# First mixture's loop: places' parts and late constants ahead of the wait for low activations, bias rows at the sixth scattering

## The chip, the cores and the metric

One core of a Trainium2 chip runs the whole program in one launch. The metric is device microseconds of that core, the median over runs. A profiled execution gives its own time, its span and a trace of every engine: PE (TensorE matmuls), PEld (its weight loads), DVE (VectorE), ACT (ScalarE), POOL (GpSimd) and the DMA queues.

## The reference

The program is a decoder of four layers over a batch of 8 sequences of 128 tokens with 128 features (1024 tokens). Each layer is an attention or recurrence, then a feed-forward part, each with layer norm and a gated residual. The change is in the feed-forward part of the first layer, a mixture of 8 experts in which each token goes to one expert:

```python
def _L0_ffn_ref(x, Wr, br, W1, b1, W2, b2):
    xf = x.reshape(-1, D)
    expert_idx = jnp.argmax(xf @ Wr.T + br, axis=-1)
    h = jax.nn.relu(jnp.einsum('td,efd->etf', xf, W1) + b1[:, None, :])
    y = jnp.einsum('etf,edf->etd', h, W2) + b2[:, None, :]
    return y[expert_idx, jnp.arange(xf.shape[0])].reshape(B, S, D)
...
x = x + jnp.tanh(g_xattn[0]) * _L0_xattn_ref(_layernorm(x), ...)
x = x + jnp.tanh(g_ffn[0]) * _L0_ffn_ref(_layernorm(x), ...)
```

The hidden width is 512. After this part come the second layer's attention and six more parts, which the change does not touch.

## The kernel before

The engines' programs are written out by hand, each in its own order, and joined by semaphores. An engine runs its own list in order, so an instruction that waits holds back everything that stands behind it in the list.

In the first mixture the tokens are sorted by expert into 15 tiles of 128 slots (1920 slots; each expert's last tile may be partly empty). Values are split into a high and a low fp16 piece, and a product is three matmuls (high by high, high by low, low by high). What matters of it:

- **Places and parts.** DVE compares each token's place with the slot numbers and so writes a 0/1 matrix for a chunk of 512 slots, in eight parts, one for each batch (`pick_dve`, L1373; its result is `PICK`, two buffers). There are four chunks, the last of 384 slots. PE multiplies the tokens' rows by the parts (`gather_pe`, L1415): for each chunk eight matmuls for the high pieces and eight for the low ones. The matmul of the high pieces for batch b waits for part b. ACT copies the result out (`gather_act`, L1423). Chunks 0 and 1 are made before the loop, 2 and 3 in it.
- **The loop over 15 tiles.** Turn i has on PE: the second layer of tile i (`tile_down_pe`, 12 matmuls), the scattering of tile i - 2 back to token order (`tile_scatter_pe`, 16 matmuls into two PSUM banks that collect all tiles), the first layer of tile i + 3 (`tile_up_pe`, 12 matmuls), and in turns 3, 4, 7 and 8 one half of a gathering (`GATHER_AT`: chunk 2 in turns 3 and 4, chunk 3 in turns 7 and 8). All but the gathering have the line of the helper `products`, L228.
- **ACT in turn i:** the high piece of tile i's result (`tile_y_act`, L1482), four relu's of tile i + 3 (L1453) and their high piece (L1458), and in the turns of `GATHER_AT` the copy of the gathered half.
- **DVE in turn i:** the low piece of tile i's result (`tile_y_dve`, L1486), the 0/1 matrix by which tile i is scattered (`put_dve`, L1401), a group of late constants in the turns of `LATE_AT` (`late_dve`, L352 to L390: high and low pieces of weights and biases and masks, most of them for later stages), the low piece of tile i + 3's activations (`tile_low_dve`, L1462), which waits for ACT's high piece, and behind it, in turns 0 to 7, two parts of `pick_dve`.
- **Second-layer bias.** PE adds it for all tokens at once, ahead of the first scattering (turn 2): 16 matmuls of 8 rows on `B2H` and `B2L`. They wait for `b_split` at 3, which group 0 of the late constants brings (L355 to L358, turn 1).

Of the kernel before, what the change touches and what calls it, by code (L numbers as in the profile page):

```python
# [8 lines left out]
NB, S, D = 8, 128, 128  # L9
TOK = NB * S  # L10
HALF = TOK // 2
F0, E0 = 512, 8
# [5 lines left out]
TILES = TOK // 128 + E0 - 1  # L18
# [22 lines left out]
def gated_mix_program(nc, t, out):  # L41
# [5 lines left out]
    with ctx:  # L47
        def sb(name, shape, dt=fp32):
            return ctx.enter_context(nc.sbuf_tensor(name, shape, dt))
# [3 lines left out]
        def sem(name):  # L53
            if name not in sems:
                sems[name] = ctx.enter_context(nc.semaphore(name))
            return sems[name]
# [36 lines left out]
        B2F, B2H, B2L = sb("B2F", [E0, D]), sb("B2H", [E0, D], fp16), sb("B2L", [E0, D], fp16)  # L93
# [5 lines left out]
        CT = sb("CT", [128, TOK], fp16)  # L99
# [32 lines left out]
        def bank(i, n=1):  # L132
            return PS[:, 512 * i:512 * (i + n)]
# [91 lines left out]
        def products(pe, dst, pairs, start=True, stop=True):  # L225

            for i, (l, r) in enumerate(pairs):
                last = pe.matmul(dst, l, r, start=start and i == 0, stop=stop and i == len(pairs) - 1)  # L228
            return last
# [66 lines left out]
        def weights_low(eng, n, q):  # L296

            eng.wait_ge(sem("s_w_high"), 4 * n + q + 1)
            if n == 1:
                eng.wait_ge(sem("s_w"), 2 + q)  # L300
            hi, lo = (w[:, quarter(q), :].rearrange("p e n -> p (e n)") for w in ((W1H, W1L), (W2H, W2L))[n])
            signal = "s_w_pool" if n == 0 and q < 2 else "s_w"
            eng.tensor_tensor(lo, staged(n, q), hi, ALU.subtract).then_inc(sem(signal), 1)
# [976 lines left out]
        def part(c):  # L1280
            return min(512, SLOTS - 512 * c)
# [25 lines left out]
        def rows_dve(dve):  # L1307
            for i in range(2):
                h = slice(4 * i, 4 * i + 4)
                dve.wait_ge(sem("s_copied"), i + 1)  # L1310
                dve.tensor_tensor(XNL[:, h, :], XN[:, h, :], XNH[:, h, :], ALU.subtract).then_inc(sem("s_row_low"), 1)

        def places_dve(dve):

            at = [ROUTED]

            def step(ins):
                at[0] += 1
                ins.then_inc(sem("r0_step"), 1)
                dve.wait_ge(sem("r0_step"), at[0])  # L1320

            step(dve.tensor_tensor(R_LESS, over(IOTA[:], E0), along(IOTA[:], E0), ALU.is_lt))
            dve.wait_ge(sem("s_ranks"), 1)
            step(dve.tensor_tensor(R_OVER, along(bank(2)[:, 0:E0], 8), over(IOTA[:], E0), ALU.is_gt))
            step(dve.tensor_reduce(R_N, R_OVER, AX, ALU.add))
            step(dve.tensor_tensor(R_SUM, over(R_N, E0), R_LESS, ALU.mult))
            step(dve.tensor_reduce(R_AT, R_SUM, AX, ALU.add))
            ranks = bank(3)[:, 0:NB * E0].rearrange("p (b e) -> p b e", b=NB)
            step(dve.tensor_tensor(R_RANK, ranks, over(R_AT, NB), ALU.add))
            step(dve.tensor_tensor(R_OWN, R_RANK, CW[:, :, 0:E0], ALU.mult))  # L1330
            step(dve.tensor_reduce(R_POS, R_OWN, AX, ALU.add))
            assert at[0] == POSITIONS

        def tiles_dve(dve):

            at = [POSITIONS]

            def step(ins):
                at[0] += 1
                ins.then_inc(sem("r0_step"), 1)  # L1340
                dve.wait_ge(sem("r0_step"), at[0])

            dve.wait_ge(sem("ld_late"), 16 * len(LATE))
            step(dve.tensor_tensor(R_TILE, over(R_AT, 16), along(SLOT[:, 0:16], E0), ALU.is_lt))
            step(dve.tensor_reduce(R_EX, R_TILE, AX, ALU.add))
            step(dve.scalar_tensor_tensor(R_EXF, R_EX, -1.0, SLOT[:, 16:32], ALU.add, ALU.mult))
            step(dve.tensor_reduce(R_SUM8, R_EXF.rearrange("p (g t) -> p g t", g=2), AX, ALU.add))
            dve.tensor_copy(R_EXI, R_SUM8).then_inc(sem("r0_step"), 1)
            assert at[0] == EXPERTS - 1

        def bias_dve(dve):

            dve.tensor_scalar(R_OH, R_EX[0:E0], 1 / 128, SLOT[0:E0, 0:1], ALU.mult, ALU.is_equal).then_inc(sem("r0_step"), 1)
# [11 lines left out]
        def pick_dve(dve, c, batches=range(NB)):  # L1365

            if c == 1:
                dve.wait_ge(sem("s_w_pool"), 2)
            if c >= 2:
                dve.wait_ge(sem("s_gathered"), 2 * c - 2)  # L1370
            n = part(c)
            for b in batches:
                dve.tensor_scalar(PICK[c % 2][:, b, 0:n], STEP[:, 0:n], 4.0 * c, R_POS[:, b:b + 1], ALU.add, ALU.is_equal)\  # L1373
                    .then_inc(sem("s_pick"), 1)
# [20 lines left out]
        def put_dve(dve, i):  # L1395

            if i >= 2:
                dve.wait_ge(sem("s_scattered"), i - 1)
            else:
                dve.wait_ge(sem("s_copied"), 5 + NB)  # L1400
            dve.tensor_scalar(PUT[:, i % 2, :], PLACE, SLOT[:, i:i + 1], None, ALU.is_equal).then_inc(sem("s_put"), 1)  # L1401
# [58 lines left out]
        def tile_low_dve(dve, i):  # L1460
            dve.wait_ge(sem("s_high"), i + 1)
            dve.tensor_tensor(LOWS[i % 3], RH[i % 3], HIGHS[i % 3], ALU.subtract).then_inc(sem("s_low"), 1)  # L1462
# [21 lines left out]
        def tile_y_dve(dve, i):  # L1484
            dve.wait_ge(sem("s_y_high"), i + 1)
            dve.tensor_tensor(YL[:, i % 2, :], bank(4 + i % 2)[:, 0:128], YH[:, i % 2, :], ALU.subtract)\  # L1486
                .then_inc(sem("s_y_low"), 1)

        def tile_scatter_pe(pe, i):

            if i == 0:
                pe.wait_ge(sem("r_ct"), 1)
                pe.wait_ge(sem("b_split"), 3)
                for b in range(NB):
                    products(pe, bank(b // 4)[:, 128 * (b % 4):128 * (b % 4) + 128],
                             [(CT[0:E0, 128 * b:128 * b + 128], b2[:]) for b2 in (B2H, B2L)], start=b % 4 == 0, stop=False)
            pe.wait_ge(sem("s_put"), i + 1)
            pe.wait_ge(sem("s_y_low"), i + 1)
            for b in range(NB):
                last = products(pe, bank(b // 4)[:, 128 * (b % 4):128 * (b % 4) + 128],  # L1500
                                [(PUT[:, i % 2, 128 * b:128 * b + 128], y[:, i % 2, :]) for y in (YH, YL)],
                                start=False, stop=i == TILES - 1 and b % 4 == 3)
                if i == TILES - 1 and b % 4 == 3:
                    last.then_inc(sem("y_turned"), 1)
            if i < TILES - 1:
                last.then_inc(sem("s_scattered"), 1)

# [46 lines left out]
                    gather_act(act, *GATHER_AT[i])  # L1554

        GATHER_AT = {3: (2, (0,)), 4: (2, (1,)), 7: (3, (0,)), 8: (3, (1,))}
        LATE_AT = (1, 4, 5, 6, 8, 9, 10, 11, 12)

        def moe0_dve(dve):
            rows_dve(dve)  # L1560
            places_dve(dve)
            pick_dve(dve, 0)
            tiles_dve(dve)
            bias_dve(dve)
            for q in (2, 3):
                weights_low(dve, 0, q)
            pick_dve(dve, 1)
            for q in range(3):
                weights_low(dve, 1, q)
            tile_low_dve(dve, 0)  # L1570
            weights_low(dve, 1, 3)
            tile_low_dve(dve, 1)
            tile_low_dve(dve, 2)
            for i in range(TILES):
                tile_y_dve(dve, i)
                put_dve(dve, i)
                if i in LATE_AT:
                    late_dve(dve, LATE_AT.index(i))
                if i + 3 < TILES:
                    tile_low_dve(dve, i + 3)  # L1580
                if i < 8:
                    at = 2 * (i % 4)
                    pick_dve(dve, 2 + i // 4, range(at, at + 2))

        def moe_loads(sp, m):
            if m == 0:
# [987 lines left out]
```

## Time and profile before

| | |
|---|---|
| Median of 3 runs | 644.99 us (644.38 to 647.12) |
| Profiled execution: time, span | 648.96 us, 647.2 us |
| Busy share: PE, DVE, ACT, POOL | 88%, 80%, 53%, 39% |
| Mean granted clock of TensorE | 0.959 of full speed |
| Loop over tiles, by PE | 74.3 to about 129 us |

The page gives the span in 40 slices of 16.2 us; the loop lies in slices 5 to 8. A row of the timeline gives the start, the duration, the engine, the line, the operation, output and inputs, how many instructions of the sort lie together, and in brackets how long the engine was idle before it and what ended the idle time. PE's durations overlap one another, so PE's pace is read from the distance of starts.

### The profile page before, as it was taken

Reading aid. Unit: us, or ns where it says so; the run is one execution under the profiler, and the core shown is the slowest. Engines: PE = TensorE matmul, PEld = TensorE weight load, DVE = VectorE, ACT = ScalarE, POOL = GpSimd, SP = SyncE. Lnnn points to the kernel's source line nnn. Section 1 sums busy time; section 2 is a strip of 40 time slices with the busy share of each in tenths; the row PEclk is TensorE's granted clock in tenths of the full one; section 3 lists DMA queues with packets and bytes.
Section 4 is the critical chain, followed back from the end, with each engine's and each line's share of the span. In section 5 each row is a group of like instructions: output and inputs, shape, how many; then the busy total and the mean of one; then the engine's idle time right before and its main releaser. Section 6 shows DMA issues by size and latency. Waiting matters only on the chain.

```text
span 647.2 us, 16313 instructions
## 1 busy us (share of the span) xinstructions
PE 567.3 (88%) x5394; PEld 292.8 (45%) x5394; DVE 518.1 (80%) x1136; ACT 340.5 (53%) x675; POOL 249.4 (39%) x456
## 2 busy tenths in 40 slices
PE   4899888987977789967999999999999779996897
PEld 2444567834653345533444344343434325553443
DVE  6798845696889868856799999999999796766886
ACT  4778735664654533433455555555555454333554
POOL 3474000210584068773244444344443100234462
PEclk9999978996998999987899999999999899997999
DMA  8500200060000000001466665666666000001110
GB/s 324 196 2 2 68 3 3 2 151 2 4 2 1 2 1 3 2 3 36 134 180 172 168 172 171 166 177 178 177 169 170 27 2 2 2 3 30 31 53 34
DMA packets 34912, 48.89 MB, mean 76 GB/s; under 512 B 6756, under 2 KB 26800, under 8 KB 34472
## 3 DMA queue, kind: packets, MB, share of 16 engines
q1 hardware_dynamic: 34424, 47.40, 25.8%
q8 instruction: 37, 0.61, 0.4%
q10 hardware_dynamic: 432, 0.73, 0.3%
q14 instruction: 19, 0.16, 0.1%
HBM read 47.29 MB, written 0.82 MB: 74 GB/s over the span
## 4 chain that ended last, share of the span: by engine, by line
PE 43%; DVE 41%; ACT 7%; issue 4%; POOL 3%; DMA 1%; DVEq 0%; ACTq 0%; SPq 0%; POOLq 0%
PE PS L228 30%; DVE PS L1115 8%; DVE SHARED L1264 4%; DVE SHARED L1788 4%; PE PS L2020 2%; DVE PS L1128 2%; ACT SHARED L1093 2%; PE PS L2026 2%; ACT SHARED L1064 2%; PE PS L1892 2%; DVE MB L1914 2%; DVE PS L1914 2%; DVE STAT L394 2%; DVE REC L2034 1%; DVE XN L410 1%
## 5 line engine op out<-in xcount | busy, mean ns | idle before, releaser
L228 PE MATMUL PS<-XH,UH 128*128 128x512 f16 x232 | 91.0, 392 | 5.4 <-DVE PS L1115 3.3
L1093 ACT ACTIVATE SHARED<-PS 128x512 f16<-128x512 f32 x96 | 57.1, 597 | 72.5 <-DVE PS L1128 67.7
L228 PE MATMUL PS<-XL,UH 128*128 128x512 f16 x232 | 90.1, 389 | 0.0
L228 PE MATMUL PS<-XH,UL 128*128 128x512 f16 x232 | 90.0, 388 | 0.0
L2001 ACT ACTIVATE SHARED<-PS 128x512 f32<-128x512 f32 x96 | 52.1, 594 | 64.0 <-PE PS L228 48.8
L228 PE MATMUL PS<-SHARED,DNH 128*128 128x512 f16 x232 | 69.0, 379 | 4.6 <-DVE SHARED L1264 3.7
L1064 ACT ACTIVATE SHARED<-PS 128x512 f32<-128x512 f32 x96 | 57.2, 597 | 20.1 <-PE PS L228 15.1
L1264 DVE TENSOR_TENSOR SHARED<-PS,SHARED 128x512 f16<-128x512 f32 x96 | 62.0, 687 | 6.8 <-ACT SHARED L1093 3.4
L1022 POOL CAST DNH<-DF 128x128 f16<-128x128 f32 x58 | 19.6, 338 | 119.7 <-DMA DF<-in_down 95.0
L1128 DVE TENSOR_TENSOR PS<-PS,SHARED 128x512 f32<-128x512 f32 x92 | 59.7, 695 | 3.8
L1115 DVE TENSOR_TENSOR PS<-SHARED,PS 128x1024 f32<-128x1024 f32 x46 | 56.6, 1230 | 6.7 <-PE PS L228 0.7
L1914 DVE TENSOR_REDUCE MB<-PS 128x4 f16<-128x512 f32 x64 | 41.1, 688 | 17.0 <-PE PS L228 11.0
L2005 POOL TENSOR_TENSOR SHARED<-SHARED,GPT 128x512 f32<-128x512 f32 x32 | 40.0, 1273 | 24.3 <-ACT SHARED L2001 24.3
L1781 ACT ACTIVATE SHARED<-PS,LOB,LOM 128x512 f16<-128x512 f32 x48 | 35.4, 775 | 26.0 <-PE PS L228 26.0
L228 PEld LDWEIGHTS PS<-XH,UH 128*128 128x128 f16 x232 | 23.1, 99 | 50.8 <-DVE PS L1115 24.6
L228 PE MATMUL PS<-SHARED,DNL 128*128 128x512 f16 x116 | 44.1, 380 | 0.0
L1015 POOL TENSOR_TENSOR UL<-UF,UH 128x256 f16<-128x256 f32 x58 | 38.9, 671 | 4.6
L2020 PE MATMUL PS<-SHARED,ONE 128*32 128x128 f32 x768 | 40.5, 284 | 0.0
L2026 PE MATMUL PS<-SHARED,V 128*32 128x128 f32 x768 | 39.4, 277 | 0.6 <-POOL SHARED L2005 0.6
L1788 DVE SCALAR_TENSOR_TENSOR SHARED<-PS,BQK,SHARED 128x512 f16<-128x512 f32 x48 | 33.6, 740 | 6.0 <-ACT SHARED L1781 5.9
L228 PEld LDWEIGHTS PS<-SHARED,DNH 128*128 128x128 f16 x232 | 22.2, 98 | 33.6 <-issue 7.1
L228 PEld LDWEIGHTS PS<-XH,UL 128*128 128x128 f16 x232 | 23.2, 100 | 29.1 <-issue 3.0
(345 smaller groups left out, 1285.8 us busy)
## 6 DMA issues: line engine op xcount, KB each, us to landing
SHARED<-w_rows_dram SPq DMA_DIRECT2D x31, 384.0 KB, 3.7
SHARED<-w_rows_dram SPq DMA_DIRECT2D x30, 256.0 KB, 3.7
UF<-in_up SPq DMA_DIRECT2D x58, 128.0 KB, 3.4
SHARED<-w_rows_dram SPq DMA_DIRECT2D x31, 128.0 KB, 2.9
DF<-in_down SPq DMA_DIRECT2D x58, 64.0 KB, 2.9
V<-in_up SPq DMA_DIRECT2D x2, 1024.0 KB, 8.3
SHARED<-in_down SPq DMA_DIRECT2D x4, 512.0 KB
SHARED<-t_values_dram SPq DMA_DIRECT2D x2, 1024.0 KB, 10.4
```

Of the source, the lines that this page charges most:

```text
L228: last = pe.matmul(dst, l, r, start=start and i == 0, stop=stop and i == len(pairs) - 1)
L1064: act.activation(SG1[u][:, hf, :], bank(hf), ACT.Silu).then_inc(sem("e_act"), 1)
L1093: act.activation(HHI[:, u, hf, :], bank(4 + hf) if m == 1 else HF[:, hf, :], ACT.Copy).then_inc(sem("e_high"), 1)
L1115: dve.tensor_tensor(dst, SG1[u].rearrange("p i n -> p (i n)"), bank(2, 2), ALU.mult).then_inc(sem("w1_gated"), 1)
L1128: dve.tensor_tensor(bank(4 + hf), bank(4 + hf), WB[u][:, HALF * hf:HALF * hf + HALF], ALU.mult)\
L1264: dve.tensor_tensor(HLO[:, u, hf, :], src, HHI[:, u, hf, :], ALU.subtract).then_inc(sem("e_low"), 1)
L1788: dve.scalar_tensor_tensor(dst, proj_bank(a, "kq", e), BQK[:, a, "qk".index(c), g:g + 1], TLO[:, e % 4, :], ALU.add, ALU.subtract).then_in ...
L1914: dve.tensor_reduce(dst, src, AX, ALU.max, negate=True).then_inc(sem("a_max"), 1)
L2001: act.activation(PF[:, j, :], bank(2 + j % 2), ACT.Exp).then_inc(sem("a_exp"), 1)
L2005: pool.tensor_tensor(PG[:, j, :].rearrange("p (g s) -> p g s", g=4), PF[:, j, :].rearrange("p (g s) -> p g s", g=4), over(GPT[:, b, :], 4) ...
L2020: pe.matmul(bank(4 + u)[32 * g:32 * g + 32, 128:256], ONE8[:, j, :], PF[:, j, 128 * g:128 * g + 128], start=j == 0, stop=j == 3, skip_grou ...
L2026: last = pe.matmul(bank(4 + u)[32 * g:32 * g + 32, 0:128], V32[:, b, 4 * g + j, :], src[:, j, 128 * g:128 * g + 128], start=False, stop=j ...
```

## The change

DVE's parts move from the end of a turn to the place between `put_dve` and the late constants, that is ahead of `tile_low_dve` and its wait. They are dealt out 3, 3 and 2 over turns 0 to 2 (chunk 2) and over turns 4 to 6 (chunk 3), in place of 2 in each of turns 0 to 7. The first four groups of late constants move from turns 1, 4, 5 and 6 to turns 3, 4, 6 and 7; the other five stay. On PE the bias matmuls move from ahead of the first scattering (turn 2) to behind the sixth (turn 7), with their waits; the first scattering now opens the two banks, and the sixth signals the end of its last bias matmul.

```diff
         def tile_scatter_pe(pe, i):
-            if i == 0:
-                pe.wait_ge(sem("r_ct"), 1)
-                pe.wait_ge(sem("b_split"), 3)
-                for b in range(NB):
-                    products(pe, bank(b // 4)[:, 128 * (b % 4):128 * (b % 4) + 128],
-                             [(CT[0:E0, 128 * b:128 * b + 128], b2[:]) for b2 in (B2H, B2L)], start=b % 4 == 0, stop=False)
             pe.wait_ge(sem("s_put"), i + 1)
             pe.wait_ge(sem("s_y_low"), i + 1)
             for b in range(NB):
                 last = products(pe, bank(b // 4)[:, 128 * (b % 4):128 * (b % 4) + 128],
                                 [(PUT[:, i % 2, 128 * b:128 * b + 128], y[:, i % 2, :]) for y in (YH, YL)],
-                                start=False, stop=i == TILES - 1 and b % 4 == 3)
+                                start=i == 0 and b % 4 == 0, stop=i == TILES - 1 and b % 4 == 3)
                 if i == TILES - 1 and b % 4 == 3:
                     last.then_inc(sem("y_turned"), 1)
+            if i == 5:
+                pe.wait_ge(sem("r_ct"), 1)
+                pe.wait_ge(sem("b_split"), 3)
+                for b in range(NB):
+                    last = products(pe, bank(b // 4)[:, 128 * (b % 4):128 * (b % 4) + 128],
+                                    [(CT[0:E0, 128 * b:128 * b + 128], b2[:]) for b2 in (B2H, B2L)], start=False, stop=False)
             if i < TILES - 1:
                 last.then_inc(sem("s_scattered"), 1)
...
-        LATE_AT = (1, 4, 5, 6, 8, 9, 10, 11, 12)
+        PICK_AT = {0: (2, range(0, 3)), 1: (2, range(3, 6)), 2: (2, range(6, 8)),
+                   4: (3, range(0, 3)), 5: (3, range(3, 6)), 6: (3, range(6, 8))}
+        LATE_AT = (3, 4, 6, 7, 8, 9, 10, 11, 12)
...
                 tile_y_dve(dve, i)
                 put_dve(dve, i)
+                if i in PICK_AT:
+                    pick_dve(dve, *PICK_AT[i])
                 if i in LATE_AT:
                     late_dve(dve, LATE_AT.index(i))
                 if i + 3 < TILES:
                     tile_low_dve(dve, i + 3)
-                if i < 8:
-                    at = 2 * (i % 4)
-                    pick_dve(dve, 2 + i // 4, range(at, at + 2))
```

## Rows read from the trace of the kernel before

**Rows 1.** The page: TensorE's granted clock in 40 slices

```profile
PEclk9999978996998999987899999999999899997999
```

**Rows 2.** Waits from 60 to 130 us: who <- for whom: us, times, longest

```profile
PE PS L1415 <- DVE V L1373: 1.9, 1, 1.9
...
PE PS L1415 <- DVE SHARED L1373: 1.6, 1, 1.6
PE PS L228 <- DVE B2L L358: 1.5, 1, 1.5
```

**Rows 3.** Busy time in stretches of the loop, with the granted clock (PEclk)

```profile
core 0: us, PE busy (x) PEld busy (x) DVE busy (x) ACT busy (x) POOL busy (x), PEclk, DMA share, GB/s
80.10:85.70 5.60, 4.08 (x44) 3.92 (x45) 3.27 (x11) 0.96 (x3) 0.00 (x0) 0.70 0.01 3
85.70:91.50 5.80, 4.22 (x51) 3.01 (x49) 3.11 (x9) 3.71 (x11) 0.95 (x1) 1.00 0.00 1
91.50:97.50 6.00, 6.00 (x50) 4.56 (x50) 1.54 (x5) 2.58 (x7) 0.00 (x0) 0.72 0.01 3
97.50:104.90 7.40, 7.40 (x122) 6.91 (x121) 6.03 (x20) 5.02 (x15) 0.98 (x1) 1.00 0.01 3
104.90:113.80 8.90, 7.02 (x59) 5.12 (x57) 3.52 (x11) 4.14 (x12) 0.00 (x0) 0.81 0.01 2
```

**Rows 4.** Timeline of DVE, turns 0 to 3, a pair of chunk 3, after the loop

```profile
66.42 2.17 DVE L1373 TENSOR_SCALAR V<-QX,SHARED 128x512 f16<-128x512 f16 x8
...
76.06 0.48 DVE L1401 TENSOR_SCALAR SHARED<-SHARED,REC 128x1024 f16<-128x1024 f16 x1
78.60 0.69 DVE L1462 TENSOR_TENSOR SHARED<-SHARED 128x512 f16<-128x512 f32 x1 [2.06 <-ACT SHARED L1458]
...
80.32 0.57 DVE L352 CAST WH<-WF 128x804 f16<-128x804 f32 x1
...
81.60 0.67 DVE L1462 TENSOR_TENSOR SHARED<-SHARED 128x512 f16<-128x512 f32 x1
...
90.63 0.61 DVE L1373 TENSOR_SCALAR SHARED<-QX,SHARED 128x512 f16<-128x512 f16 x2
...
98.21 0.55 DVE L1373 TENSOR_SCALAR V<-QX,SHARED 128x384 f16<-128x384 f16 x2
...
129.09 0.75 DVE L1697 SCALAR_TENSOR_TENSOR X<-PS,G,X 128x512 f32<-128x512 f32 x1 [1.58 <-PE PS L228]
```

**Rows 5.** Timeline of PE: a whole gathering, turn 2, the halves' first six matmuls

```profile
69.09 3.62 PE L1415 MATMUL PS<-V,CF 128*128 128x512 f16 x16
...
78.96 0.22 PE L228 MATMUL PS<-W2H,SHARED 128*128 x1
...
81.62 0.21 PE L228 MATMUL PS<-B2H,CT 8*128 8x128 f16 x1 [1.53 <-DVE B2L L358]
...
87.99 1.47 PE L1415 MATMUL PS<-SHARED,CF 128*128 128x512 f16 x6
...
104.85 1.14 PE L1415 MATMUL PS<-V,CF 128*128 128x384 f16 x6
```

**Rows 6.** Busy time in single turns without gathering (6, 7 but its gathering, 9, 11)

```profile
99.71:102.29 2.58, 2.58 (x44) 2.33 (x41) 2.17 (x8) 2.02 (x6) 0.98 (x1) 1.00 0.04 10
102.29:104.85 2.56, 2.56 (x41) 2.32 (x41) 2.56 (x10) 2.05 (x6) 0.00 (x0) 1.00 0.00 0
113.77:116.01 2.24, 2.24 (x43) 2.23 (x40) 0.80 (x2) 0.97 (x3) 0.00 (x0) 1.00 0.00 0
...
118.51:121.24 2.73, 2.70 (x44) 2.35 (x41) 2.49 (x12) 2.05 (x6) 0.00 (x0) 1.00 0.02 6
```

**Rows 7.** Timeline of ACT: the high piece of tile 4

```profile
80.18 0.63 ACT L1458 ACTIVATE SHARED<-SHARED 128x512 f16<-128x512 f32 x1
```

**Rows 8.** The chain that ended last: products of turns 0 and 1

```profile
74.32 1.19 PE PS L228 x12
...
75.65 1.09 PE PS L228 x12
```

## The prediction

> **What bounds the kernel now.** I looked first at the page's slices of the granted clock [rows 1]: within the loop over tiles the clock is not full in slices 5, 6 and 7. Then I asked for the waits of that stretch. PE has three there that end with a DVE instruction, 1.9, 1.6 and 1.5 us [rows 2]: one on the low piece of the second-layer bias, two on a part of a chunk. The timeline says where. The bias matmul starts at 81.62 after 1.53 us of idleness; the gathering of chunk 2 does six matmuls at 87.99 and then stands, and that of chunk 3 does six at 104.85 and stands [rows 5]. In both it is the last pair of parts, the one of turn 3 (DVE at 90.63) and the one of turn 7, that is late [rows 4]. Last I cut the loop into stretches [rows 3]. PE is idle 5.60 - 4.08 = 1.52, 5.80 - 4.22 = 1.58 and 8.90 - 7.02 = 1.88 us in three of them, 4.98 together, and not at all in the others. The clock is at 0.70, 0.72 and 0.81 in 80.1 to 85.7, 91.5 to 97.5 and 104.9 to 113.8, and 1.00 between. With the two levels of 1.2 and 2.4 GHz, 0.70 over 5.60 us is 3.36 us at the lower level, 0.72 over 6.00 is 3.36, and 0.81 over 8.90 is 3.38. Each came just after one of the three idle times, and each loses half its length: 1.68 + 1.68 + 1.69 = 5.05 us.
>
> So in the loop PE is the bound wherever it is not waiting, and DVE is the one that it waits for, though DVE itself is idle much of the time: it stood 2.06 us in front of the low piece of tile 3 [rows 4], with two parts queued behind, and the parts needed nothing that was late. An in-order queue has put work that is ready behind a wait.
>
> **The change part by part.**
>
> *Bias to the sixth scattering.* The wait of 1.53 us before the first scattering goes. What then holds the first scattering? Its matrix was written at 76.06 + 0.48 [rows 4] and the low result before that, so nothing: PE goes on from tile 2's second layer, begun at 78.96 [rows 5], at about 80.1. The 16 matmuls are no fewer: at full clock I take the pace of the turns, below, about 0.055 us each, 0.9 us together, in turn 2 or in turn 7 alike; this term is zero. The new place waits for `b_split` from turn 3 of DVE, four turns earlier: no wait. Behind it stand tile 10's first layer and the high half of chunk 3, 0.9 us later than otherwise, which only helps the parts.
>
> *Parts ahead of the low piece.* Eight parts of 512 slots took 2.17 us, 0.27 each; a pair of 384 slots 0.55 or less, so 0.24 to 0.27 each [rows 4]. In turn 0 three parts go from 76.5 to 77.3, into the idle 2.06 us before 78.60: free. In turn 1 DVE writes result and matrix from 79.2 to 79.8 and three parts to 80.6; the high piece of tile 4 ends at 80.81 [rows 7], so free again, and its low piece comes at 80.9, earlier than the 81.60 of now. In turn 2 the result waits for the first scattering, about 81.0; DVE takes it at 81.5 and ends the last two parts at 82.7. PE meanwhile: second layer of tile 2 to 80.1, scattering 81.0, first layer 81.8, turn 3 in some 2.6 us [rows 6] to 84.4, then the gathering. The seventh part is wanted six matmuls later, at 84.4 + 6 x 0.22 = 85.7 (16 took 3.62 us [rows 5]). Margin: 3.0 us. The second stall goes, 1.58.
>
> For chunk 3 the parts lie in turns 4 to 6. DVE gets to turn 6's result about 2.9 us after PE begins that turn (PE's turn of 2.6, then relu's and high piece hold the low piece before it), and ends two parts 0.6 + 0.5 us later, at +4.0. PE begins the gathering of turn 7 at 2.6 + 2.6 + 0.9 (bias) = +6.1, so the seventh part has a margin of over 2 us. The third stall goes, 1.88.
>
> *Late constants.* Group 0 lasts from 80.32 to 81.60, 1.28 us [rows 4], and now stands in turn 3 in front of the low piece of tile 6, which PE wants three turns later. DVE's heaviest turns become 4 and 6, with 0.2 + 0.4 (result, matrix) + 0.7 or 0.5 (parts) + about 1 (constants) + 0.6 (low piece) = 2.9 us at most, against PE turns of 2.6 + 1.8 and 2.6. The excess of 0.3 us in turn 6 is covered by turns 5 and 7, which have less on DVE and more on PE. Cost 0; were the cover gone, 0.3 us.
>
> *Clock.* With no idle time in this stretch, the three falls should not come. This is where I choose: the stretch 97.5 to 104.9, PE busy without a gap, kept 1.00 [rows 3], and so I take the whole 5.05 for the profiled execution. The lower bound is 0.
>
> *The sum,* first way: 1.52 + 1.58 + 1.88 + 5.05 = 10.0. Second way, a walk over turns 2 to 8: the turns without a gathering last 2.58, 2.56, 2.24 and 2.73 [rows 6]; their mean is 2.53, times seven 17.7; the half gatherings 1.8 + 1.8 + 1.4 + 1.4 = 6.4 (a chunk of 384 at three quarters); bias 0.9. That is 25.0, so turn 9 starts at 78.96 + 25.0 = 104.0 where it starts at 113.77 now [rows 6]: 9.8. With all turns at 2.24 it is 11.8, with all at 2.73 8.4. I take 9.8: the profiled 648.96 would be 639.2. The end of the loop has nothing of fixed time: from turn 9 all engines follow PE, and the next attention begins when the last scattering ends.
>
> The median of the timed runs is 4.0 us under the profiled execution, so some idle or low-clock time of this trace may be missing in them. The stalls are of the order of the queues and stay, 5.0; of the clock's 5.05 I count five sixths, 4.2. Gain 9.2: **644.99 - 9.2 = 635.8**.
>
> *A rule against it.* Two of the four turns of [rows 6] give 2.58 and 2.73 us for 40 matmuls, 65 to 68 ns each. The Trainium skill (TensorE: Matmul & The Clock Gate, Back-to-back issue gap) gives about 81 ns for a sustained stream of matmuls of 128 columns. By that figure a turn would be an estimated 3.2 us and seven turns some 5 us longer; the trace does not agree in any turn at full clock.
>
> **The rivals.**
>
> *A. The clock stays low.* The falls come from the thin stretches of short products in the loop and not from the gaps. For: 0.70 began while PE had been working again for some time. Against: 97.5 to 104.9, the same work, at 1.00 [rows 3]. Gain 5.0: 640.0. The same page (Why this matters for your kernels) ties a fall to gaps longer than these three; by it they would not be the cause.
>
> *B. PE's own pace.* With no stalls, PE never finds its instructions lying ready. In turns 0 and 1, 24 matmuls with weights picked by register took 1.19 + 1.09 us, 95 ns each [rows 8]. If all seven turns went so, one would last 2.28 + 0.9 (scattering) = 3.18 us, 0.65 more than the mean, 4.5 in all. Gain 9.8 - 4.5 = 5.3: 639.7. Against: turns 6 and 7 follow each other without a stall, at 2.58 and 2.56 [rows 6].
>
> *C. The third stall stays,* because DVE, with constants and parts before each low piece, falls behind in turns 4 to 6. Gain 10.0 - 1.88 - 1.69 = 6.4: 638.6. It wants a delay of over 2 us where I find 0.3.
>
> *D. Given back:* the loop ends sooner and the next stage waits for something of its own, or falls in other places for the clock. 643 to 646.
>
> *E. Slower.* The parts now stand between the high piece and the low piece of each tile; if the second layer wants the low piece at once, 8 x 0.27 + 8 x 0.24 = 4.1 us come onto the path and a wait on low pieces takes the place of each stall: 649.1. It decides where the low piece ends later than PE reaches the tile. Tile 3's ends at 79.3 and PE comes for it at 81.8, so 2.5 us would have to be lost against parts of 0.8.
>
> **How the numbers follow.** My forecast (633 to 638.2) 0.66, A 0.12, B 0.08, C 0.06, D 0.04, E 0.04. About 0.5%, 3.2 us, is what a measurement of this kernel can tell from no change. Faster by more than that: 0.66 + 0.12 + 0.08 + 0.06 = 0.92, less 0.02 for a run of small misses: 0.90; same 0.06; slower 0.04. The range goes from 632.5 (turns at the quick pace, all falls gone) to 641.0, which takes in A, B and C and leaves out D and E and 0.1 for the rest.
>
> **What the profile after would show.** PE without a wait on L1373 or L358 in the loop; a granted clock of 1.00 from 74 to about 119; DVE's parts ahead of L1462 in turns 0 to 2 and 4 to 6; the last gathering ending near 103.5 and the first L1697 near 119.3 in place of 129.1 [rows 4]. I am wrong if PE waits for L1462 (E), if parts are still late in turn 7 (C), if the clock falls between 80 and 105 with no gap before it (A), or if turns last 3 us at full clock (B).

## The result and the profile after

The changed kernel takes 636.99 us (635.60 to 639.53, 4 runs) against 644.68 us (644.38 to 647.12, 4 runs): ratio 0.9887, 95% interval 0.9853 to 0.9920. The profiled execution took 636.67 us with a span of 634.9 us. Six more runs in a second comparison gave 637.07 us and a ratio of 0.9904 (0.9868 to 0.9939).

The page of the changed kernel, the granted clock; slices are 15.9 us here, the loop lies in slices 5 to 8:

```profile
PEclk9999999987998799979999999999999899997999
```

The low slices within the loop [rows 1] are gone. The same loop in stretches (columns as in [rows 3]; from the scattering of turn 2 to the gathering of turn 3; that gathering and turns 4 and 5; turns 6 to 8 with chunk 3; the rest):

```profile
80.36:84.51 4.15, 4.15 (x69) 3.79 (x67) 3.09 (x10) 3.07 (x9) 0.00 (x0) 1.00 0.02 6
84.51:92.43 7.92, 7.92 (x99) 6.03 (x97) 6.16 (x19) 5.14 (x14) 1.32 (x1) 1.00 0.01 3
92.43:104.20 11.77, 11.77 (x168) 10.01 (x166) 8.87 (x26) 8.29 (x25) 1.06 (x1) 1.00 0.01 3
104.20:119.10 14.90, 14.90 (x228) 13.13 (x226) 10.17 (x26) 8.52 (x24) 4.37 (x4) 1.00 0.01 2
```

PE is busy in every microsecond from 80.4 to 119.1. Where [rows 3] have 4.08 of 5.60 and 7.02 of 8.90, stretch and busy time are now one number, and the clock is 1.00. Of PE's waits from 74 to 119 us [rows 2] this is all that is left; it is the wait for the second layer's weights that stands ahead of the loop in both kernels:

```profile
PE PS L228 <- DVE SHARED L303: 1.0, 1, 1.0
```

DVE's timeline, turns 0 to 2 and the turns with chunk 3, answers to [rows 4]:

```profile
76.77 0.87 DVE L1373 TENSOR_SCALAR SHARED<-QX,SHARED 128x512 f16<-128x512 f16 x3
78.91 0.69 DVE L1462 TENSOR_TENSOR SHARED<-SHARED 128x512 f16<-128x512 f32 x1 [1.27 <-ACT SHARED L1458]
...
80.12 0.87 DVE L1373 TENSOR_SCALAR SHARED<-QX,SHARED 128x512 f16<-128x512 f16 x3
81.16 0.69 DVE L1462 TENSOR_TENSOR SHARED<-SHARED 128x512 f16<-128x512 f32 x1 [0.17 <-ACT SHARED L1458]
...
82.37 0.61 DVE L1373 TENSOR_SCALAR SHARED<-QX,SHARED 128x512 f16<-128x512 f16 x2
...
85.55 1.04 DVE L355 CAST BH<-BF 4x128 f16<-4x128 f32 x1
...
92.93 1.54 DVE L1373 TENSOR_SCALAR V<-QX,SHARED 128x384 f16<-128x384 f16 x3
...
95.67 0.54 DVE L1373 TENSOR_SCALAR V<-QX,SHARED 128x384 f16<-128x384 f16 x2
...
119.15 0.75 DVE L1698 SCALAR_TENSOR_TENSOR X<-PS,G,X 128x512 f32<-128x512 f32 x1 [1.58 <-PE PS L228]
```

DVE still waits for ACT, 1.27 us in turn 0 where it was 2.06, but nothing that PE needs soon is queued behind. The last pair of chunk 2 is ready at 83.0 and its first part wanted at about 85.8; the last pair of chunk 3 is ready at 96.2 and wanted at about 99.6. Two rows were not expected, a cast of 4 x 128 of 1.04 us and three parts in 1.54 us; they come back below.

I measure the loop from the first matmul of tile 0's second layer to DVE's first update of x. Before it is 74.32 to 129.09, 54.77 us; after, 74.63 to 119.15, 44.52 us. That is 10.25 us in the traced executions, against some 7 in the medians. Where the rest went is what the experiments are about.

### The profile page after: what moved, and what is told of

The parts are those of the page before. It is cut to its first block, busy times and chain, and to the rows that moved or that the text cites. A ratio compares the mean times of both kernels' runs of the same rounds, so it can differ in the third digit from the quotient of the medians.

```text
span 634.9 us, 16313 instructions
## 1 busy us (share of the span) xinstructions
PE 562.7 (89%) x5394; PEld 289.0 (46%) x5394; DVE 518.2 (82%) x1136; ACT 340.1 (54%) x675; POOL 249.3 (39%) x456
## 4 chain that ended last, share of the span: by engine, by line
PE 44%; DVE 41%; ACT 6%; issue 4%; POOL 3%; DMA 1%; DVEq 0%; ACTq 0%; POOLq 0%
PE PS L228 29%; DVE PS L1115 9%; DVE SHARED L1264 5%; DVE SHARED L1789 4%; DVE PS L1128 3%; PE PS L2021 2%; ACT SHARED L1093 2%; PE PS L2027 2%; DVE MB L1915 2%; ACT SHARED L1064 2%; PE PS L1893 2%; DVE REC L2035 1%; DVE PS L1915 1%; DVE STAT L394 1%; DVE XN L410 1%
```

## The experiments

A row of the whole loop gives its length, PE's busy time and the granted clock at once. All such rows below have the columns of [rows 3].

### The kernel before, traced twice more; the changed one once more

Unaltered code. What was expected, for the second and third trace of the kernel before and for the second of the changed one:

> The kernel before, unaltered, traced again. If each wait brings a fall of the clock by itself: the same three waits (1.5, 1.6, 1.9 us), the same three stretches at the lower clock, loop 54.8. If it depends on how the wait falls in the execution: the same three waits, but only some of the falls, loop 49.7 plus 1.7 for each fall that is there.

> As the run before this, a third trace of the kernel before: three waits again; 49.7 plus 1.7 us for each fall of the clock that is there.

> The changed kernel once more, unaltered, timed against the kernel before in five rounds. The traces so far show waits of 1.6 to 1.9 us on PE with a fall of the clock behind them (kernel before) and without one (bias alone, chunk 3 late). If the three waits are a fixed gain of 5.0 us and the clock's part a matter of the single execution, the ratio is 0.987 to 0.989 (7 to 8.5 us), the loop again takes 44.4 to 44.6 us without a wait, and the span less its clock loss is 4.5 to 5 us shorter than that of the kernel before. If the profiled 10.2 us of the loop were the whole truth: ratio 0.984.

Second trace of the kernel before, the whole loop and two stretches that hold the first two waits:

```profile
74.14:124.59 50.45, 45.19 (x614) 36.97 (x615) 30.85 (x88) 29.40 (x83) 6.30 (x6) 1.00 0.07 24
...
79.90:83.60 3.70, 2.18 (x39) 2.09 (x39) 2.68 (x9) 0.72 (x3) 0.00 (x0) 1.00 0.02 4
83.60:90.30 6.70, 5.11 (x62) 3.61 (x59) 3.72 (x10) 4.12 (x13) 0.95 (x1) 1.00 0.00 1
```

Its waits:

```profile
PE PS L1415 <- DVE V L1373: 1.9, 1, 1.9
PE PS L1415 <- DVE SHARED L1373: 1.6, 1, 1.6
PE PS L228 <- DVE B2L L358: 1.5, 1, 1.5
```

Third trace of the kernel before, the loop:

```profile
74.83:128.03 53.20, 47.92 (x614) 39.95 (x615) 30.88 (x89) 29.39 (x83) 6.24 (x6) 0.94 0.07 22
```

Second trace of the changed kernel, the loop:

```profile
74.32:118.74 44.42, 44.13 (x614) 36.92 (x615) 32.27 (x88) 29.16 (x83) 6.72 (x6) 1.00 0.08 27
```

The three waits are the same to a tenth in every trace of the kernel before. The falls of the clock are not: three in the first trace, none in the second, two in the third, with loops of 54.77, 50.45 and 53.20 us. A fall costs (54.77 - 50.45) / 3 = 1.44 and (53.20 - 50.45) / 2 = 1.38 us. With no fall at all the kernel before needs 50.45 and the changed one 44.47 (mean of 44.52 and 44.42): **6.0 us are fixed in the loop, and 0 to 4.3 depend on the execution**. My trace of before was the worst of three.

A fall at the lower level lasts 3.4 us and so takes 1.7 us from PE, but the loop is only 1.4 longer. The two traces of the same code show where some of it comes back. The second layer of tile 3 stands right behind the first fall; these are its first matmul and the first one behind it, in the first trace and then in the second:

```profile
85.75 0.22 PE L228 MATMUL PS<-W2H,SHARED 128*128 x1
...
86.42 0.22 PE L228 MATMUL PS<-ATH,SHARED 128*128 128x128 f16 x1
```

```profile
83.99 0.22 PE L228 MATMUL PS<-W2H,SHARED 128*128 x1
...
84.96 0.22 PE L228 MATMUL PS<-ATH,SHARED 128*128 128x128 f16 x1
```

It takes 0.67 us behind the fall and 0.97 without one. From the first bias matmul to the first one of the gathering the first trace needs 87.99 - 81.62 = 6.37 us [rows 5] and the second 86.52 - 81.43 = 5.09, so this fall costs 1.28.

The traces also differ outside the loop. From the loop's end to the end of the span, the three traces of the kernel before take 518.1, 515.0 and 514.0 us and the two of the changed one 515.8 and 515.8. Part of that lies in the next stage, the second layer's attention. Its first 23 us, in the changed kernel and in the second trace of before:

```profile
119.15:142.15 23.00, 18.24 (x127) 8.01 (x124) 19.47 (x48) 12.94 (x20) 3.62 (x6) 0.93 0.43 107
```

```profile
124.59:147.59 23.00, 17.13 (x135) 7.89 (x132) 20.44 (x49) 13.37 (x21) 4.34 (x6) 1.00 0.42 107
```

The changed kernel has a fall there, in both its traces, and comes to DVE's first reciprocal of the attention 32.5 us after the loop's end (151.64) where this trace of before needs 31.6 (156.21). The first trace of before has the same fall and needs 32.3. So up to 0.9 us of the loop's gain can be given back here, depending on which execution of before one compares with.

### The waits one by one

The first, bias alone, is the kernel before with the PE part of the diff and nothing of DVE's.

> The kernel before with the bias matmuls moved to the sixth scattering and nothing else. My theory (three gaps of 1.52, 1.58 and 1.88 us, each followed by about 3.4 us at the lower clock): the first gap and the first fall go, the two waits on parts stay at 1.6 to 1.9 us with a fall each. The loop, from tile 0's second layer to the update of x (54.8 us before, 44.5 after the whole change), takes 51.3 to 51.9; the kernel gains 3.2 us. Theory A (falls do not come from the gaps): three falls stay and the loop takes 53.2; gain 1.5. If the bias move is what the whole gain hangs on: loop near 44.5.

```profile
74.64:123.69 49.05, 45.29 (x614) 37.02 (x615) 30.86 (x89) 29.41 (x83) 6.32 (x6) 1.00 0.07 24
```

642.54 us, ratio 0.9979 (0.9951 to 1.0007). The first wait is gone, the other two are there (1.6 and 1.9 us), and in this execution there was no fall, where I expected two. The loop is 1.40 us shorter than 50.45. The gain of 3.2 us that I expected is the very end of the interval, which takes in no gain at all.

The second, parts alone, is the kernel before with `PICK_AT` as in the change; `LATE_AT` and the bias stay.

> The kernel before with the parts moved ahead of the late constants and the low piece; bias and late constants where they were. My theory: the two waits on parts go with their falls, 1.58 + 1.88 + 3.37 = 6.8 us; the wait for the bias pieces grows, because three parts now stand before them in turn 1, from 1.5 to about 2.2 us; the loop takes 48.5 to 49, the kernel gains 6.0 to 6.4. Theory A: gain 2.8 at most. If the parts do not hold PE: no gain.

```profile
74.24:121.64 47.40, 45.32 (x614) 38.30 (x615) 31.39 (x88) 29.03 (x83) 6.36 (x6) 0.96 0.07 25
```

641.30 us, ratio 0.9953 (0.9923 to 0.9982). Both waits on parts are gone, and that for the bias has grown from 1.5 to 1.8 us, not to 2.2; one fall follows it. The loop is 7.4 us under the first trace of before, but 3.05 under the second, with a fall that the second has not. The median's gain of 2.5 us (3.0 by the ratio) is far under the 6.0 to 6.4 that I expected. That figure took two falls of the first trace as certain, 3.4 us. It does not explain everything, since the loop alone, by the ladder below, would give 2.10 + 2.48 - 0.3 = 4.3 us without any fall; in this trace the stages behind the loop took 518.1 us, 3 more than in the second trace of before.

The third is the changed kernel with only chunk 3 put back:

```diff
-        PICK_AT = {0: ..., 1: ..., 2: ..., 4: (3, range(0, 3)), 5: (3, range(3, 6)), 6: (3, range(6, 8))}
+        PICK_AT = {0: ..., 1: ..., 2: ...}
...
                 if i + 3 < TILES:
                     tile_low_dve(dve, i + 3)
+                if 4 <= i < 8:
+                    pick_dve(dve, 3, range(2 * (i - 4), 2 * (i - 4) + 2))
```

> The changed kernel with chunk 3's parts alone put back behind the low piece, two in each of turns 4 to 7. My theory: one wait of 1.5 to 1.9 us comes back in turn 7, and with it one stretch of 3.4 us at the lower clock, 1.7 us: the loop takes 47.7 to 48.2 in place of 44.5, the kernel loses 3.2 to 3.6 us against the changed one. If PE could make the wait good later (slack behind it): loss under 1 us.

```profile
74.21:121.16 46.95, 44.79 (x614) 36.95 (x615) 31.58 (x88) 29.33 (x83) 6.63 (x6) 1.00 0.08 25
```

639.24 us, ratio 0.9936 (0.9911 to 0.9961). The wait of 1.9 us is back, without a fall in this execution, and the loop is 2.48 us longer than 44.47; 47.7 to 48.2 was expected with a fall.

All at full clock, these make a ladder (the step to "chunk 3 late" also moves the late constants):

| kernel | waits in the loop | loop, us | step, us | idle time of the wait |
|---|---|---|---|---|
| before (second trace) | three | 50.45 | | |
| bias alone | two on parts | 49.05 | 1.40 | 1.52 |
| chunk 3 late | the last | 46.95 | 2.10 | 1.58 |
| changed | none | 44.47 | 2.48 | 1.88 |

The two waits on parts cost 0.5 and 0.6 us more than PE's idle time shows. PE's timeline shows where; first the kernel before (second trace) around the wait in chunk 2, up to the scattering behind tile 4's second layer:

```profile
86.52 1.46 PE L1415 MATMUL PS<-SHARED,CF 128*128 128x512 f16 x6
89.58 0.65 PE L1415 MATMUL PS<-SHARED,CF 128*128 128x512 f16 x2 [1.59 <-DVE SHARED L1373]
90.06 0.22 PE L228 MATMUL PS<-W2H,SHARED 128*128 x1
...
91.01 0.22 PE L228 MATMUL PS<-ATH,SHARED 128*128 128x128 f16 x1
```

The same in the changed kernel:

```profile
84.51 1.89 PE L1415 MATMUL PS<-SHARED,CF 128*128 128x512 f16 x8
86.24 0.22 PE L228 MATMUL PS<-W2H,SHARED 128*128 x1
...
86.91 0.22 PE L228 MATMUL PS<-ATH,SHARED 128*128 128x128 f16 x1
```

The gathering takes 3.54 us from start to start against 1.73: 1.81, 0.2 more than the idle time, because the last matmul before a gap is shown with its full duration (six take 1.46 us, and 1.30 by the distance of starts of 0.216). Tile 4's second layer then takes 0.95 us against 0.67. Its matmuls pick their weights by register; they run fast where eight long matmuls stand in front of them, and not where only two do.

### The gaps filled with work

The first lines are in `tile_scatter_pe`, the others in `gather_pe`, where the idle matmuls first wait for a step of ACT (`s_relu`):

```diff
             if i == 0:
+                fill_pe(pe, 0, 6)
                 pe.wait_ge(sem("r_ct"), 1)
...
+                    if i == 0 and c >= 2 and b == 6:
+                        pe.wait_ge(sem("s_relu"), (20, 36)[c - 2])
+                        fill_pe(pe, (3, 7)[c - 2], (6, 7)[c - 2])
                     if i == 0:
                         pe.wait_ge(sem("s_pick"), NB * c + b + 1)
```

> The kernel before with 6, 6 and 7 idle matmuls of 512 columns (0.22 us each) put in front of its three waits on PE, into banks that nothing reads afterwards. All three waits stay as long as they are, only PE works through most of them. My theory: the granted clock stays 1.00 throughout the loop, which gives back the clock's part alone, 5.0 us: loop 49.5 to 50. Theory A (falls do not come from the gaps): the clock falls as before, loop 54.8, gain 0.

```profile
74.08:124.70 50.62, 49.43 (x633) 38.77 (x634) 30.86 (x88) 29.37 (x83) 6.39 (x6) 1.00 0.07 24
```

642.02 us, ratio 0.9963 (0.9932 to 0.9994). The waits are still there for DVE, the loop is as long as in the second trace of before (50.62 against 50.45), and only the falls can have gone. So the trace alone proves nothing, as a trace without falls came without filling too. The timed runs do speak: over 12 executions against 35 of before, the clock's share is worth 1.75 us in the medians, 0.4 to 4.4 by the interval, where 5.0 was expected. The mean granted clock leans the same way, 0.9656 in the changed kernel's ten runs against 0.9627 in 63 runs of before, which is 0.0029 of some 640 us, 1.9 us. But it is no second proof: it counts the whole program, and two kernels below that have no wait in the loop either had 0.9620 and 0.9592 in four runs each, against 0.9612 for the kernel before in the same comparison.

### How much can stand ahead of the low piece

All 16 parts in turn 0, and then each written twice, to move rival E's threshold:

```diff
-                if i in PICK_AT:
-                    pick_dve(dve, *PICK_AT[i])
+                if i == 0:
+                    pick_dve(dve, 2)
+                    pick_dve(dve, 3)
```

> The changed kernel with all 16 parts of chunks 2 and 3 in turn 0, in one row ahead of the low piece of tile 3. Eight parts of 512 at 0.29 us and eight of 384 at 0.26 end at about 81.1, the low piece at 81.7; PE wants it at 81.9 in the changed kernel. My theory: it still fits, the loop takes 44.5 to 44.9. The rival that I called E (parts between high and low piece come onto the path) would add up to 4.3 us and a fall of the clock: 49 to 50.

> The same with each of the 16 parts written twice in turn 0 (double work, the same values). The low piece of tile 3 now ends 4.4 to 5.5 us later than in the run with 16, at 86.1 to 87.2, and PE wants it at 81.9. My theory of the threshold (a part costs nothing until the low piece ends later than PE reaches the tile, then all of it): PE stands 4.2 to 5.3 us for the low piece in turn 3 and runs 3.4 us at the lower clock, loop 50.5 to 52. If DVE had hidden slack for it: loop near 44.5.

With 16, DVE's timeline and the loop:

```profile
76.61 2.19 DVE L1373 TENSOR_SCALAR SHARED<-QX,SHARED 128x512 f16<-128x512 f16 x8
78.70 1.92 DVE L1373 TENSOR_SCALAR V<-QX,SHARED 128x384 f16<-128x384 f16 x8
80.54 0.69 DVE L1462 TENSOR_TENSOR SHARED<-SHARED 128x512 f16<-128x512 f32 x1
```

```profile
74.45:118.92 44.47, 44.18 (x614) 36.96 (x615) 31.46 (x88) 29.24 (x84) 6.61 (x6) 1.00 0.09 27
```

Written twice, PE's timeline and the loop:

```profile
86.12 0.27 PE L228 MATMUL PS<-W2H,SHARED 128*128 x1 [4.04 <-DVE ATL L1486]
```

```profile
74.73:125.68 50.95, 46.62 (x614) 39.06 (x615) 35.67 (x104) 29.30 (x83) 6.62 (x6) 0.93 0.07 23
```

Sixteen parts cost nothing (638.50 us, ratio 0.9925, 0.9902 to 0.9948): the low piece ends at 81.2 and tile 1's result behind it at 81.4, and PE begins tile 3 at 81.8. Twice as many cost 4.04 us of waiting and a fall (0.93 over 50.95 us is some 7 us at the lower level, twice as long as the falls of the kernel before), 6.5 us of the loop (643.15 us, ratio 0.9980, 0.9959 to 1.0001), which is nearly the whole gain of the change. The wait is put down to tile 1's result (L1486), which stands directly behind the low piece on DVE and is wanted by the same matmul. So E's mechanism is real, and its threshold lies at about 4.5 us of parts in turn 0; the change puts 0.9 there.

### The bias left out, and the scattering halved

> The changed kernel without its 16 bias matmuls: the second layer's bias is left out of the result. My theory prices them at 0.9 us on PE, so the loop takes 43.6. If they are hidden, 44.5.

```profile
74.37:117.71 43.34, 43.05 (x598) 36.00 (x599) 32.17 (x89) 29.12 (x83) 6.74 (x6) 1.00 0.09 28
```

The 16 bias matmuls cost 1.13 us on PE behind the sixth scattering: 1.0 from their first start to that of the next layer (96.99 to 97.98 in the changed kernel), and 0.1 in the scattering in front of them, which takes 0.99 instead of 0.89. In turn 2 of the kernel before (second trace) they take 0.98; what leaving them out there would give was not run. 636.28 us, ratio 0.9877 (0.9857 to 0.9896).

```diff
                 if i >= 2:
-                    tile_scatter_pe(pe, i - 2)
+                    tile_scatter_pe(pe, i - 2, range(0, 4))
                 if i + 3 < TILES:
                     tile_up_pe(pe, i + 3, ex[i + 3])
+                if i >= 2:
+                    tile_scatter_pe(pe, i - 2, range(4, 8))
```

> The changed kernel with each scattering cut in two: the first four batches ahead of the first layer of tile i + 3, the other four behind it, so that the 24 matmuls with weights picked by register no longer stand in one row. Theory of PE's own pace: the turns of 2.5 to 2.7 us at full clock are longer than 2.24 because such matmuls come no faster than 80 to 95 ns when they stand in a row; with static ones between them a turn takes 2.24 to 2.35, and the loop gains 1.5 to 3 us: 41.5 to 43. The rival: the pace is that of each kind for itself or of the engines around, the turns stay at 2.5, loop 44.5 or up to 0.5 more, because ACT's copy of the result waits for the second half.

```profile
74.25:120.89 46.64, 45.97 (x614) 37.37 (x615) 32.58 (x88) 27.94 (x83) 6.55 (x6) 1.00 0.08 26
```

638.38 us, ratio 0.9912 (0.9892 to 0.9933). My theory of this one fell: the loop is 2.2 us longer, PE's busy time 1.8. The other 0.4 is the rival's: PE waits 0.36 us at 105.91 for ACT's copy of the gathered half (L1423). PE's timeline in turn 3, the third matmul of each group of three of tile 6's first layer, with eight static matmuls in front:

```profile
83.22 0.22 PE L228 MATMUL PS<-SHARED,W1L 128*128 128x128 f16 x1
83.45 0.22 PE L228 MATMUL PS<-SHARED,W1L 128*128 128x128 f16 x1
```

and in the changed kernel, with sixteen:

```profile
83.95 0.22 PE L228 MATMUL PS<-SHARED,W1L 128*128 128x128 f16 x1
84.12 0.22 PE L228 MATMUL PS<-SHARED,W1L 128*128 128x128 f16 x1
```

Three matmuls take 0.23 us against 0.17. What counts seems to be how long a stretch of static work stands in one piece, and halving it leaves two that are too short; why this is so is not shown. I know of no version here that beats the changed kernel.

### GpSimd's memsets moved

```diff
                 for b in (2, 3):
-                    pool.wait_ge(sem("s_put"), 2 * b)
+                    pool.wait_ge(sem("s_put"), 2 * b + 1)
```

> The changed kernel with GpSimd's two memsets of 1024 columns waiting for one scattering matrix more (the 5th and 7th in place of the 4th and 6th). In the changed kernel DVE's cast of 4 x 128 takes 1.04 us beside the first memset (0.21 in the kernel before) and three parts of turn 5 take 1.54 in place of 0.77 beside the second. If the two engines hold each other up: the cast takes 0.21 and the parts of turn 5 take 0.77 again, and whatever DVE does beside the memsets in their new place is longer by up to 0.8. If it is the instructions' own: 1.04 and 1.54 stay. The loop stays at 44.5 either way, since DVE's slack covers both.

DVE's timeline:

```profile
85.64 0.21 DVE L355 CAST BH<-BF 4x128 f16<-4x128 f32 x1
...
89.09 1.54 DVE L1373 TENSOR_SCALAR V<-QX,SHARED 128x384 f16<-128x384 f16 x3
...
93.05 0.77 DVE L1373 TENSOR_SCALAR V<-QX,SHARED 128x384 f16<-128x384 f16 x3
...
95.79 1.32 DVE L1373 TENSOR_SCALAR V<-QX,SHARED 128x384 f16<-128x384 f16 x2
```

GpSimd's, in the changed kernel and then with the memsets moved:

```profile
85.20 1.32 POOL L277 MEMSET V<- 128x1024 f32 x1 [27.76 <-DVE SHARED L1401]
93.07 1.06 POOL L277 MEMSET V<- 128x1024 f32 x1 [6.55 <-DVE SHARED L1401]
```

```profile
89.23 1.06 POOL L277 MEMSET V<- 128x1024 f32 x1 [31.50 <-DVE SHARED L1401]
95.93 1.06 POOL L277 MEMSET V<- 128x1024 f32 x1 [5.64 <-DVE SHARED L1401]
```

The long instructions went with the memsets: the cast is back at 0.21, and the parts beside the memsets at 89.2 and 95.9 take 0.8 us more. In the changed kernel the long cast, begun at 85.55, ends at 86.59, as the memset does at 86.52. The loop is 44.49 us; DVE's slack covers it. This is one run. The Trainium skill (SBUF — State Buffer, SBUF: two separate sides) says that DVE, in its modes that use two ports, and GpSimd take one pair of ports in turn, and the later one stands until the other's instruction is over; the trace agrees in the end times, 86.59 against 86.52; that these casts and comparisons run in such a mode is inferred, no trace names the mode.

## Why the prediction was right, and where it was not

Forecast 635.8 us, 632.5 to 641.0, faster with 0.90. Measured 636.99. The mechanism was right, and two sizes in the sum were wrong in opposite directions. By its own steps:

- **The three waits and their causes** were as read: each went with the part of the change that was named for it (bias alone, chunk 3 late, parts alone).
- **The term of the waits, 5.0 us, was too small.** It measured 6.0, the ladder's sum. Idle time understates the two gaps on parts by 0.5 to 0.6 us each. The walk over turns, which does not go by idle time, gave 25.0 us for turns 2 to 8; in the changed kernel they took 103.50 - 79.28 = 24.2, 17.2 in the turns (17.7 foreseen), 6.1 in the half gatherings (6.4) and 1.0 in the bias (0.9).
- **The term of the clock was mis-sized, and this was the larger error.** "Of the clock's 5.05 I count five sixths, 4.2" rested on one trace in which all three falls came. For "five sixths" the prediction had no row; it had seen that the medians lay 4.0 us under the profiled execution, and took only 0.85 off for it. Three traces show three falls, none and two, 2.35 us in the mean, and the runs with filled gaps put the worth at 1.75 us, with a wide interval. A fall is also worth 1.4 us and not 1.68, since the register-picked matmuls behind it make up some of the lost time (0.30 us in tile 3's second layer).
- **The sum,** 6.0 + 1.75 = 7.75 us, against 644.68 - 636.99 = 7.7 (7.3 by the ratio; 6.2 by that of the second comparison, whose interval of 3.9 to 8.5 takes in 7.75). The forecast of 9.2 was 1.5 too high: -2.45 in the clock, +1.0 in the waits. That the sum closes so well is luck, with 1.75 known to no better than 0.4 to 4.4. So is it that the first way's 10.0 came so near the 10.25 of the traced pair: there the waits were worth 5.9 against 4.98, and the falls 4.3 against 5.05.
- **Nothing else on the path.** "The last gathering ending near 103.5" came at 103.50 (the prediction's own walk says 104.0 for the same place), "the first L1697 near 119.3" at 119.15 (now L1698). That these were so close in the traced execution is in part luck: the trace of before and the profile after were at the two ends of what the clock does.
- **DVE's margins** were right for turns 0 to 2 (the last part at 83.0, foreseen 82.7). For turn 6 I found +4.0 us and it is 95.67 + 0.54 - 92.43 = 3.8, though the parts of turn 5 took twice their time beside the memset, which I had not priced.
- **Rivals.** A, falls that do not come from the gaps: none of the six traces of kernels without a wait in the loop, nor the filled one, has a fall there, and every fall seen in the loop begins in a gap or within 2 us behind one, so in this loop the gaps are needed; but a gap of 1.5 to 1.9 us is not enough by itself: of 13 in six traces, 6 were followed by a fall. B, PE's own pace: its turns of 2.55, 2.58 and 2.65 us stay in the band of [rows 6]. C did not come. E was made to happen and needs five times the parts. D did not come at its price of 643 to 646, but in a small way it may have: the fall in the next stage, up to 0.9 us. The medians cannot settle so little.

The Trainium skill (TensorE: Matmul & The Clock Gate, Why this matters for your kernels) ties a fall to gaps longer than these. The traces agree so far that gaps of 1.5 to 1.9 us can pass without one, and disagree in that five of nine such gaps in three traces of the kernel before were followed by one.

## What to carry to other kernels

In an in-order queue, put work that has all its inputs ahead of a wait, and size the room by when the consumer of the waiting instruction really comes, not by the wait. Here 0.9 us of parts went in free, 4.1 us did too, and 8.2 us cost 4.0 of waiting and 6.5 of the loop. Price a gap on PE by where the work behind it starts and how fast it goes, not by idle time alone. And trace the kernel before more than once ahead of counting a clock's falls in a sum: the waits repeat to a tenth, the falls do not.

## What the hardware showed that I had not expected

- The same code with the same three gaps on PE ran its loop with three falls of the granted clock, none, or two: 54.77, 50.45, 53.20 us.
- A GpSimd memset of 1024 columns (0.95 us at the least, 1.06 and 1.32 beside these) holds up DVE's fp16 comparisons and casts: a cast of 4 x 128 took 1.04 in place of 0.21 us, three parts of 384 1.54 in place of 0.77. It followed the memset when that was moved.
- The first twelve matmuls with weights picked by register come 0.06 us apart behind sixteen static ones or eight long ones. The next twelve in the same row, and mostly those behind only eight static ones, come 0.08 apart. Splitting the static stretch in two cost 2.2 us of the loop.
